# Attention 2 of a four-part kernel: when the loads, the token sums, the maxima units and the projection fronts are issued

## What is computed

```python
x = x + attn0(layernorm(x))        # one head over each batch
x = x + ffn0(layernorm(x))         # 12 experts, top 3, then a factor per batch
x = x + attn1(layernorm(x))        # 16 heads of 16, 4096 stored keys and values
x = x + ffn1(layernorm(x))         # 8 experts, top 2, and a shared one

# end of ffn0: the factor
pooled = out.mean(axis=1)                                    # per batch, over tokens
phi = sigmoid(relu(pooled @ Wp1 + bp1) @ Wp2 + bp2)
return out * (1.0 - (phi > 0.7) * 0.8)

# attn1
Q = (query @ Wq.T).reshape(B, QL, 16, 16)
scores = einsum('bqhd,khd->bhqk', Q, K) * SCALE
attn = softmax(scores); out = einsum('bhqk,khd->bqhd', attn, V).reshape(B, QL, 256)
return out @ Wo.T
```

## Time and profile before

| | |
|---|---|
| median of 3 runs | 2128.39 us (2121.38 to 2128.75) |
| the profiled execution | 2126.7 us |
| its span, first to last instruction | 2125.0 us |
| TensorE busy | 1972.1 us (93%) |
| VectorE busy | 1559.6 us (73%) |
| ScalarE busy | 1346.0 us (63%) |
| POOL busy | 334.3 us (16%) |
| granted TensorE clock, mean | 0.947 |

### The profile page before, as it was taken

One profiled execution on the slowest core, in us unless ns is written; L12 is line 12 of the kernel. 1 busy time (PEld: TensorE's weight loads), 2 busy tenths in 40 slices (PEclk: granted clock), 3 DMA queues, 4 the chain that ended last, 5 costly groups with the idle time before them and its releaser, 6 DMA issues. The chain is left out here.

```text
span 2125.0 us, 40519 instructions
## 1 busy us (share of the span) xinstructions
PE 1972.1 (93%) x15964; PEld 999.5 (47%) x15964; DVE 1559.6 (73%) x2056; ACT 1346.0 (63%) x2652; POOL 334.3 (16%) x333
## 2 busy tenths in 40 slices
PE   6993999997669999999999999999999999998995
PEld 3653889996323333333333333333333333356673
DVE  2537112223689999999999999999999999823454
ACT  1220444441037878888888888888888888764321
POOL 0001334431310100000000000000000000002473
PEclk9995999997569999999999999999999999989997
DMA  4202768865811313103212103222102000001135
GB/s 147 94 21 71 228 221 263 256 212 152 116 19 17 58 46 41 21 11 41 30 33 29 20 14 37 30 37 24 20 17 84 8 9 9 17 26 38 43 102 168
DMA packets 168417, 150.45 MB, mean 71 GB/s; under 512 B 89594, under 2 KB 136678, under 8 KB 167462
## 3 DMA queue, kind: packets, MB, share of 16 engines
q1 hardware_dynamic: 158822, 122.16, 24.8%
q0 software_dynamic: 9408, 25.70, 3.8%
HBM read 108.30 MB, written 32.37 MB: 66 GB/s over the span
## 5 line engine op out<-in xcount | busy, mean ns | idle before, releaser
L1102 DVE TENSOR_REDUCE maxp<-banks 128x2 f32<-128x1024 f32 x1024 | 1224.0, 1220 | 35.0 <-PE banks L1096 34.6
L1813 ACT ACTIVATE pring<-banks 128x512 f32<-128x512 f32 x2048 | 1110.9, 597 | 208.2 <-PE banks L1678 91.2
L1693 PE MATMUL banks<-pring,vcur 128*17 128x256 f32 x8192 | 644.5, 388 | 9.0 <-ACT osb L1807 8.1
L1678 PE MATMUL banks<-qst,kst 50*128 50x512 f32 x2048 | 512.3, 499 | 0.0
L1096 PE MATMUL banks<-kst,qst 50*128 50x512 f32 x2048 | 425.3, 413 | 34.7 <-DVE maxp L1102 18.6
L1678 PEld LDWEIGHTS banks<-qst,kst 50*128 50x128 f32 x2048 | 192.5, 185 | 431.5 <-ACT pring L1813 409.2
L1693 PEld LDWEIGHTS banks<-pring,vcur 128*17 128x17 f32 x8192 | 139.1, 96 | 376.5 <-issue 200.3
L1096 PEld LDWEIGHTS banks<-kst,qst 50*128 50x128 f32 x2048 | 198.6, 191 | 64.4 <-DVE maxp L1102 46.0
L822 ACT ACTIVATE hT<-banks,b 128x128 f32<-128x128 f32 x295 | 107.8, 367 | 188.6 <-PE banks L758 173.8
L960 DVE TENSOR_SCALAR yo<-banks,wblock 128x256 f32<-128x256 f32 x59 | 28.5, 484 | 225.0 <-PE banks L767 225.0
L1650 POOL TENSOR_TENSOR osb<-osb,pairs 64x512 f32<-64x512 f32 x31 | 39.5, 1274 | 727.2 <-DMA pairs<-osb 727.2
(11 more groups left out here) (330 smaller groups left out, 1269.8 us busy)
## 6 DMA issues: line engine op xcount, KB each, us to landing
w1r<-in_L_ffn_w SPq DMA_DIRECT2D x59, 640.0 KB, 4.9
kst<-key_parts SPq DMA_DIRECT2D x18, 512.0 KB
key_parts<-ksp SPq DMA_DIRECT2D x32, 256.0 KB, 2.9
w2all<-in_L_ffn_w SPq DMA_DIRECT2D x12, 640.0 KB, 8.1
qst<-query_parts SPq DMA_DIRECT2D x90, 64.0 KB
kf<-in_kT SPq DMA_DIRECT2D x16, 256.0 KB, 5.6
vcur<-in_v SPq DMA_DIRECT2D x16, 256.0 KB, 9.1
yb<-expert_rows SPq DMA_DIRECT2D x8, 512.0 KB, 7.4
```

The source lines that it names most:

```text
L1102: return nc.vector.tensor_reduce(maxp[:, :, hp, qt, kb], ps[:, base:base + 2, :], X, ALU.max)
L1678: nc.tensor.matmul(ps[:, score_bank(n), :], kst[g % 2][rows, h, kt * P:(kt + 1) * P], qst[i][rows, h, :], start=True, stop=True).then_inc( ...
L1693: mm = nc.tensor.matmul(ps[VR * j:VR * j + VC, 7, cols], vcur[g % 2][:, 2 * m + j // 2, 2 * h + j % 2, :], pring[:, (G % 2) * HG + j, cols ...
L1813: nc.scalar.activation(pring[:, n % (2 * HG), :], ps[:, score_bank(n), :], ACT.Exp, scale=float(DH) ** -0.5).then_inc(exp_done, 1)
```

## The change

Five things are done.

1. Batch 0's token sums are made from the added tiles, tile by tile, as those of the other batches; the 32 products over raw rows and `bias_summed` go. Batch 2's sums move from maxima units 14 and 15 to units 3 to 6, batch 3's to one tile each in units 14 to 17, with banks and takes (`TAKE_POOLED`) of their own.
2. SP issues the other three quarters of the keys after sums 2, and sums 3 after them, all in front of the copies that place the queries.
3. `EARLY` is 2 instead of 6, and stage 0's units are spread over steps 0 to 12.
4. `FRONTS`: batch 0 goes to stage 29, batch 1 to stage 30 (two products among the maxima, the rest in the last four steps), batch 2 stays in stage 31 and is spread wider.
5. SP's `store_rows` and POOL's `norm_pool` follow the fronts.

```diff
-                POOLED, POOLED_BANK = {14: (2, 0), 15: (2, 2), 16: (3, 0), 17: (3, 2)}, 0
+                POOLED = {u0 + i: (c, i) for c, u0 in ((2, 3), (3, 14)) for i in range(TB)}
+                POOLED_BANK = {2: 2, 3: 0}
+                TAKE_POOLED = {8: 2, 18: 3}
...
                         load_keys(sp, 0, 0, keys_in0, slice(0, FEW))
-                        for c in range(1, NB):
-                            load_sums(sp, c)
+                        load_sums(sp, 1)
+                        load_sums(sp, 2)
+                        load_keys(sp, 0, 0, keys_in1, slice(FEW, KEYS))
+                        load_sums(sp, 3)
                         sp.wait_ge(q_split, 1)
                         for s in range(2):
                             place_queries(sp, 0, s)
                         sp.wait_ge(q_left, 1)
                         place_queries(sp, 0, 2)
-                        load_keys(sp, 0, 0, keys_in1, slice(FEW, KEYS))
...
-                        for k in range(-1, TOP0):
-                            if k >= 0:
-                                pe.wait_ge(first_in[k], 16)
-                            for i in range(TB):
-                                rows = acc[:, i] if k < 0 else expert_sums[0][:, k, i]
-                                for m in range(KD):
-                                    mm = nc.tensor.matmul(ps[:, 2 + m, 0:1], rows[:, m * P:(m + 1) * P], ones[:, 0:1],
-                                                          start=(k < 0 and i == 0), stop=(k == TOP0 - 1 and i == TB - 1))
-                            if k < 0:
-                                mm.then_inc(bias_summed, 1)
+                        for i in range(TB):
+                            mm = pool_tokens(0, i, 2)
                         mm.then_inc(pooled_mm, 1)
...
                                     if i == TB:
                                         pe.wait_ge(main.taken, KD * (b + 1))
-                                        pe.wait_ge(q_left, KD)
+                                        pe.wait_ge(pooled_done, 3)
...
                             if c == 0:
                                 dve.wait_ge(first_in[TOP0 - 1], 16)
-                                ch(nc.vector.tensor_tensor(acc[:, tiles, :], acc[:, tiles, :], expert_sums[c][:, TOP0 - 1], ALU.add))
-                                return
                             for i in range(TB):
...
-            FRONTS = [[11, 12, 14, 15, 16], [17, 18, 20, 21, 22], [23, 24, 27, 28, 29]]
+            FRONTS = [[-14, -12, -7, -5, -3], [2, 4, 12, 13, 14], [18, 20, 24, 26, 28]]
...
-                    begin, end = H * NM - (AHEAD if H else 0), (H + 1) * NM - AHEAD
+                    begin, end = H * NM - (AHEAD if H else 0), (H + 1) * NM - (AHEAD if H else 3)
...
-            EARLY = 6
+            EARLY = 2
...
-                        if H == STAGES - 1:
-                            store_rows(sp, 0, NB)
+                        if H >= STAGES - 2:
+                            store_rows(sp, H - (STAGES - 2), NB)
...
-                        if H == STAGES - 2:
-                            norm_pool(pool, NB + 1, main)
+                        if H >= STAGES - 4:
+                            norm_pool(pool, NB + H - (STAGES - 4), main)
```

More of the change, by code:

```diff
@@ L1344, in _ @@
                             if u in POOLED:
-                                c, i0 = POOLED[u]
-                                if (c, i0) == (2, 0):
-                                    pe.wait_ge(main.taken, 2 * KD)
-                                for i in range(i0, i0 + 2):
-                                    mm = pool_tokens(c, i, POOLED_BANK)
-                                if (c, i0) == (NB - 1, 2):
+                                c, i = POOLED[u]
+                                if i == 0:
+                                    if c == 2:
+                                        pe.wait_ge(q_left, KD)
+                                    else:
+                                        pe.wait_ge(main.taken, 2 * KD)
+                                mm = pool_tokens(c, i, POOLED_BANK[c])
+                                if i == TB - 1:
                                     mm.then_inc(pooled_mm, 1)
                             if u == FAC_HIDDEN:
-                                hidden_factor(2, 2, NB, POOLED_BANK)
+                                pe.wait_ge(pooled_done, 4)
+                                hidden_factor(2, 2, NB, 0)
                             if u == FAC_SUMMED:
-                                summed_factor(2, 2, NB, POOLED_BANK)
+                                summed_factor(2, 2, NB, 0)
                     @block.scalar
@@ L1448, in _ @@
                         add_rows(0)
-                        ch.wait()
                         factors(0, 0, 1, 2)
@@ L1468, in _ @@
                                 add_rows(ADD[u])
+                            if u in TAKE_POOLED:
+                                c = TAKE_POOLED[u]
+                                dve.wait_ge(pooled_mm, c + 1)
+                                nc.vector.tensor_scalar(pooled[:, :, c:c + 1], ps[:, POOLED_BANK[c]:POOLED_BANK[c] + KD, c:c + 1], 1.0 / S, None,
+                                                        ALU.mult).then_inc(pooled_done, 1)
                             if u in FACTOR:
[L1470 removed]
+                                factor_step(FACTOR[u], 2, 2, NB, 0)
                             if u in RESIDUAL:
```

16 lines of the change are left out of this document (4 added, 12 removed).

## The result

The changed kernel takes 2154.45 us (median of 4 runs, 2146.04 to 2161.68), the kernel before 2127.05 us beside it (4 runs). The ratio is 1.0135 (95%: 1.0116 to 1.0154): slower by 1.35%, 27 us, where the prediction had 0.4% and a range that ended at 2147. A second build of it gave 1.015 (1.0116 to 1.0184). The profiled execution is the fastest of its four, 2146.04 us (mean granted clock 0.946; the other three 0.937 to 0.942), with a span of 2144.3 us, 19.3 us above that of before. So the profile shows 19 us of the 27 us that the medians differ by.

A forecast was written before the change was run, and what follows sets the result against it. It took VectorE's maxima and TensorE, both within 6% of full, as the bound. +6.8 - 1.0 + (17.2 + 4.0 - 18.3) = +8.7 us on the profiled 2126.7 gave 2135.4 us, as median 2137; range 2122 to 2147.

The forecast's parts named there:

- Loads in front of the queries: Before stage 0: query copies wait behind the keys in SP's queue, VectorE's first reduction moves to 547.5 us, +11.3 us.
- Rival A: Before stage 0: small copies don't wait for the keys, first stretch -8.4 us, time 2122 us; chance 0.10.
- Two units ahead: Around stage 0: scores start four units earlier, the units return inside the stage; -1.0 us (+1.5 to -4.6).
- Fronts: Stages 29 to 31: front work moved among the maxima, +17.2 us, clock dips +4.0 us, last stretch -18.3 us.
- the dense part: Stages 29 and 30: added front work, batch 0 10.4 us and batch 1 6.8 us, +17.2 us, plus +4.0 us of dips.
- the router: Batch 0's router unit among the maxima: VectorE's wait of 1.15 us plus 0.34 us, 1.5 us.
- the second product: Stages 29 and 30: VectorE's wait, addition and normalisation hold the maxima, TensorE stands 3.3 us; taken as 5.0 us.
- two dips of 4.7 us: Stages 29 and 30: half clock after each stand of TensorE, a step losing 43%; +4.0 us (0 to 10).
- rival B: Stages 29 and 30: clock stays low some 12 us after each stand, 5.2 us each, 2143 us; chance 0.15.
- the tail: Last stretch, 1846.60 to 1916.38 us: seven of fifteen front units leave, 69.8 us becomes 51.5 us, -18.3 us.
- Rival C: Stages 29 and 30: engines hide each other's front work, no dip, fronts -8.7 us, 2128 us; chance 0.11.
- the first stretch: Up to stage 0: later first reduction +11.3, no key wait -1.1, one tile instead of two -3.4; +6.8 us.

The follow-up runs named there:

- again: The changed kernel, unaltered, built and profiled a second time: 2157.12 us, 1.015 of the kernel before.
- early_back: The changed kernel with loads, fronts and six maxima units ahead as in the kernel before, only the token sums left: 2118.56 us, 0.9974 of before.
- both_back: The changed kernel with both loads and fronts as in the kernel before, still two maxima units ahead: 2119.19 us, 0.9981 of before.
- loads_back: The changed kernel with only the order of the loads as in the kernel before: 2136.63 us, 1.0049 of before.
- router_late: The changed kernel with batch 0's router moved to step 12 of stage 30, batch 1's last three units one step back: 2153.79 us, 1.0142 of before.
- deferred: The changed kernel with the normalisation of batches 0 and 1 in six pieces, one behind each following reduction: 2149.85 us, 1.0126 of before.
- first two groups: The runs up to the one where ScalarE issued the remaining keys after its first exponential (2141.85 us); later runs were on two other chips.
- keys_late: early_back with the six remaining key loads issued from ScalarE's queue after the last sums landed: 2156.99 us, 1.0037 of before.
- b0_only2: early_back with batch 0's front alone moved into stage 29, repeated on one chip with others: 2153.21 us, 1.0024 of before.

## Why the prediction was wrong

**Loads in front of the queries: right.** The copies wait behind the keys. The first maximum came at 548.99 us (forecast 547.5), the first mark 7.2 us late in the profile after and 10.7 us in that of again (forecast +6.8). Rival A (the copies do not wait) is dead. By medians the part costs 0.68 to 1.0 points, 14 to 21 us; the distance between forecast and rival A was 15.2 us. That +7.2 lies so near +6.8 is in part luck. The first maximum came 1.5 us later than forecast, and VectorE's additions behind it took 3.3 us more, a collision told below. Against that, the stretch from the first maximum to the first mark shrank by 5.5 us where -4.5 was forecast, in spite of the collision (in early_back, without it, by 7.7 us). One size of the working was off without consequence: the products over the added tiles (16 instructions, 3.58 us together) release the factor at 507.08 instead of 510.88 us, 3.8 us earlier and not 5.4; either is waited away behind the keys.

**Two units ahead: no gain.** -1.0 us was forecast; both_back and early_back differ by 0.07 points in favour of six. The term lies within what the measurement can tell. After's -3.5 us from the first to the second mark is no proof of it, since the clock moves that stretch by more.

**Fronts: the step that failed.** The prediction said +17.2 + 4.0 - 18.3 = +2.9 us. The stretch from the mark of stage 29 to the end of attention 2 lasts 163.6, 164.8, 167.4 and 165.3 us in after, again, loads_back and router_late, against 145.9 to 152.0 us in the eight profiles with the fronts of before (deferred, which reorders VectorE's work too, has 161.9 us): a mean of 165.3 against 150.3, +15 us. The medians say 14 to 21 us. Term by term:

- the dense part, forecast 17.2 + 4.0 = 21.2 us: 27.8 us in after, 32.1 in again, 30.4 in loads_back. Of the 27.8 us, batch 0 has some 18 (2.4 for the first product, 6.35 for the second, some 2.6 for the transposes, 6.3 for the router, some 0.5 left for the first dip) against 10.4 and 2.0 for its dip, batch 1 the other 9.6 against 6.8 and 2.0;
- the router was the most mis-sized: forecast 1.5 us, 6.3 us measured. The prediction took VectorE's wait for a product unit, 1.15 us, and the two small copies, 0.34 us. It left out TensorE's own time for the router, 2.85 us (1.92 us in again, at full clock): VectorE waited 2.98 us for it. It also had no dip there; the 6.8 us at half clock, 2.9 us at 43%, are within the 6.3 us;
- the second product was put at 5.0 us, with some time won back, and cost 6.35 us. Stage 29 is 11.2 us longer, of which 2.4 + 6.35 + 2.0 us are these rows (2.0 for the transposes before the mark) and some 0.5 us are left for the dip of 3.4 us inside the stage. At 43% that dip is 1.5 us; so either up to 1 us was won back, as forecast, or the dip cost less. The rows do not separate the two;
- two dips of 4.7 us were forecast. After had 3.4, 6.8 and 3.4 us, again 10.0, 6.8 and 6.6 us: an estimated loss of 5.8 and 10.1 us for the forecast 4.0. In estimated time lost this is up to rival B's size (10.4 us), yet B had no dip at the router, and its 12 us each were not reached; its sign, over 8 us at 0.50 after batch 0's normalisation, is absent in after (3.4 us) and present in again (10.0 us);
- the tail, forecast -18.3 us: -16.2 in after, and by the means of the same profiles 56.8 against 71.2 us, -14.5 us. Low stretches go on there: at 1888.5 us TensorE ran for 6.8 us at 0.50, where one dip of 1.5 us in all was allowed for.

Rival C (hidden fronts, stages 29 and 30 within 13 us) is dead too. So direction and the first stretch were right, and the size of the fronts failed, by the router's price and the clock above all.

In the profile after, the forecast had 6.6 us too little in the dense part and 2.1 us too much taken off the tail, out of 10.6 us by which the profiled execution missed the forecast 2135.4. The median missed 2137 by 17 us. The prediction put it 1.7 us above the profiled execution, as in the kernel before; it lies 8.4 us above. The three other executions had lower mean clocks (0.937 to 0.942 against 0.946), and where in the program is not recorded. Behind attention 2 nothing was forecast and 3.3 us were seen in one profile; the other profiles of the first two groups show 206 to 208 us whatever the edit, and the chip can change it by some 20 us. Still open are whether loads and fronts cost more together than apart, and what decides between a dip of 3 and one of 10 us.

## What to carry to other kernels

Before moving work out of a thin tail into a full stage, ask what it costs there, with the half clock behind it and with every engine's own time for that unit, and do not take the wait from another unit or the price from the tail; here a router priced at 1.5 us cost 6.3 us, half clock included. Put work that makes an engine pause next to other independent work (the interleaved fronts won 0.29 points for a row of fifteen numbers), and keep big transfers behind the small ones that the next stage waits for. The version with the token sums over added tiles, the old load order and the interleaved fronts is the best found: 0.9943 of before.

## What the hardware showed

**Two adders on one memory.** With the loads moved, batch 2's additions on VectorE fell into the time of POOL's sums of batch 3. VectorE's timeline after, POOL's after, then VectorE's of early_back:

```profile
550.13 6.00 DVE L1384 TENSOR_TENSOR acc<-acc,pring 128x1024 f32<-128x1024 f32 x2
...
546.99 8.07 POOL L1275 TENSOR_TENSOR acc<-acc,last_rows 128x1024 f32<-128x1024 f32 x3 [8.15 <-DMA last_rows<-expert_rows]
```

```profile
534.87 2.71 DVE L1383 TENSOR_TENSOR acc<-acc,pring 128x1024 f32<-128x1024 f32 x2
```

The same two additions took 6.00 us instead of 2.71 us, right on the path between VectorE's first and second reduction. All five profiles in which POOL's additions began some 3 us before VectorE's have 5.95 to 6.00 us; keys_late, where POOL began 0.8 us after VectorE, has 4.51 us; where POOL began only after VectorE had ended, it is 2.71 us. The Trainium skill (SBUF — State Buffer, "SBUF: two separate sides") says that VectorE with two inputs in SBUF and GpSimd lock each other out for a whole instruction; the trace agrees, with 3.3 us lost. The prediction had looked for nothing here.

**The clock.** The same program shows half-clock stretches of 3.4 us (after) and 10 us (again) behind the same pause of 3.08 us, and TensorE can be busy for all of 13.5 us at 0.50 from within a router that was preceded by a pause of only 0.82 us (b0_only2). With the same code in the tail, the mean clock of 55 us was 1.00 in one profile and 0.88 in another.
